# Pairing the down products of four shared pieces behind a routed loop, and moving the count of ranks

## The chip, the cores and the metric

The kernel runs on one core of one Trainium2 chip. The metric is the device time of one execution in microseconds (us), of which several runs are taken. A profile is one further execution with the hardware profiler on. Engines are called as in the profile: PE is TensorE (PEld its weight loads), DVE is VectorE, ACT is ScalarE, POOL is GpSimd, SP is SyncE.

## What is computed

1024 tokens of width 512 (two sequences of 512) go through a feed-forward part, attention, and the same feed-forward part again, each behind a layer norm and added to the stream `x`:

```python
x = x + 0.5 * ffn(layernorm(x))
x = x + attention(layernorm(x))      # 32 heads of 128, 8 key/value heads, causal
x = x + 0.5 * ffn(layernorm(x))

# ffn: a shared part and 16 routed experts, the best 2 for each token
gu_s = x2 @ shared_w_gate_up.T;  g_s, u_s = split(gu_s)          # inner width 512
shared_out = silu(g_s) * u_s @ shared_w_down.T
probs = softmax(x2 @ gate_w.T);  topk_vals, topk_idx = top_k(probs, 2)
gu = einsum('th,eih->eti', x2, w_gate_up)                        # inner width 128
out_e = einsum('eti,ehi->eth', silu(g) * u, w_down)
ffn = combine(out_e) + shared_out
```

## The kernel before

Matrix products are made in three steps from a high and a low part of each operand (`PARTS`; the parts have the type fp32r), so that one product of 128 x 512 is three matmuls a chunk of 128 inner elements. Transposes, the down product of the experts and the count of ranks are plain fp32 matmuls, which the trace shows as two records each.

The shared part of a feed-forward stage is cut into eight **pieces** (`SLOTS`): four slices of 128 of the inner width (`NSH`) times two halves of the tokens. Piece s has slice s // 2 and token half s % 2. For each piece PE runs `gate_up(n, s)` (24 matmuls: 12 into a gate bank 0 or 1, 12 into an up bank 2 or 3), ACT takes the silu (`gate`), DVE multiplies (`multiply`), ACT and DVE cut the result in two parts (`high`, `low`), PE runs `down(n, s)` (12 matmuls into banks 4 to 7, one bank a token tile), and DVE adds the four banks to `x` (`add_down`, L934). Each `down` waits bank by bank for the `add_down` of the piece before it.

Pieces 0 to 4 (`BEFORE` = 4) begin ahead of the **routed loop**, the rest comes behind it. The routed loop works off 31 tiles of 128 rows, sorted by expert. How it gets its rows: DVE picks the two experts of each token (`router`, `chosen`); PE counts with nine matmuls against `below` and `ones` how many tokens come before each one (`rank`, L1224 and L1228, put between the second and the third of the four chunks of the up product of piece 1); DVE turns this into row numbers (`place`, L878 to L889); POOL scatters the rows with 16 indirect DMAs (L490), SP loads them tile by tile (L324), and PE transposes the first one (L1239).

Behind the loop POOL gathers the results back into `yg` with 16 indirect DMAs, two for each token tile (L501); in the first feed-forward stage it makes subtractions for the attention weights between them (L524). DVE adds them to `x` with their weights (`combine`, L1015, four instructions for two token tiles). The order on each engine is written out by hand, in `feed_forward` and what follows it. In the first stage the next norm hangs on the end of this work (`statistics`, `scaled` L827, then PE's `turn_norm` L1153); in the second stage the output is stored by SP as soon as a tile is complete.

The order behind the loop on PE, before: gate/up of 5, down 4, gate/up of 6, down 5, then down 6 and gate/up of 7 (first stage) or gate/up of 7 and down 6 (second stage), down 7. Each engine goes strictly through its list, so an instruction that waits holds what stands behind it.

## Time and profile before

| | us |
|---|---|
| median of 3 runs | 1179.36 |
| lowest and highest | 1179.07, 1181.36 |
| the profiled execution, its own time | 1182.96 |
| its span, first to last instruction | 1181.3 |
| PE busy in the span | 1116.7 (95%) |
| DVE, ACT, POOL busy | 674.8, 567.6, 469.3 |

Read it from the chain of waits, which follows the work that ended last back from the end of the program, and then in the order of time at the places where the chain leaves PE. Starts are in us from the beginning of the span. The timeline joins neighbouring instructions of one kind into a row ("x4"); its duration is that of the row. The first feed-forward stage lies at 0 to 222, attention behind it to about 984, the second stage from there to the end.

### The profile page before, as it was taken

The numbers are of one execution on the slowest core, as the hardware profiler recorded it, in microseconds if no ns is written. First come the engines' busy times: TensorE is split into PE (matmuls) and PEld (weight loads), VectorE is DVE, ScalarE is ACT, GpSimd is POOL, SyncE is SP. The second block draws the span as 40 slices with busy tenths as digits, with TensorE's granted clock in tenths as the row PEclk, the third lists the DMA queues.
The fourth block names the chain that finished last, engine by engine and source line by source line (L and its number), as shares of the span: only waits on it lengthen the run. The fifth ranks groups of instructions, "written<-read, shape, count | busy, mean of one in ns | idle before, by whom it ended". The sixth has DMA issues, their size and how long they took to land.

```text
span 1181.3 us, 20221 instructions
## 1 busy us (share of the span) xinstructions
PE 1116.7 (95%) x5982; PEld 931.3 (79%) x5983; DVE 674.8 (57%) x1826; ACT 567.6 (48%) x1512; POOL 469.3 (40%) x486
## 2 busy tenths in 40 slices
PE   5989997889999999999999999999999988989996
PEld 4867775778888888888888888888888876877774
DVE  6657768755444545455445454454544456667767
ACT  3346652356445536454545454544543543356640
POOL 1456548116315325323423532522531410455543
PEclk9999999899999999999999999999999999999999
DMA  9984556101101000010110110010100017744546
GB/s 355 388 335 165 171 173 221 54 1 37 54 2 36 35 19 5 31 53 0 36 53 0 36 53 0 36 53 0 36 1 1 1 36 272 310 146 162 171 155 190
DMA packets 38603, 114.61 MB, mean 97 GB/s; under 512 B 4384, under 2 KB 4384, under 8 KB 36512
## 3 DMA queue, kind: packets, MB, share of 16 engines
q1 hardware_dynamic: 33440, 97.30, 22.8%
q0 software_dynamic: 5120, 16.78, 4.2%
q8 instruction: 22, 0.36, 0.1%
q14 instruction: 21, 0.17, 0.0%
HBM read 79.20 MB, written 34.87 MB: 97 GB/s over the span
## 4 chain that ended last, share of the span: by engine, by line
PE 84%; DVE 5%; issue 3%; ACT 3%; DMA 3%; POOL 1%; SPq 0%; DVEq 0%; ACTq 0%; POOLq 0%
PE bank L1291 23%; PE bank L1360 15%; PE bank L1376 8%; PE bank L1326 8%; PE bank L1270 6%; PE bank L1196 6%; PE bank L1304 6%; PE bank L1278 3%; PE bank L1213 2%; PE bank L1239 2%; POOL x_rows L490 1%; PE bank L1372 1%; PE bank L1322 1%; DMA experts<-in_ffn_w 1%; DVE x L1015 1%
## 5 line engine op out<-in xcount | busy, mean ns | idle before, releaser
L517 POOL TENSOR_TENSOR scores<-scores,pinv 128x512 f32<-128x512 f32 (+3 forms) x256 | 176.4, 721 | 367.0 <-DVE pinv L1052 367.0
L467 POOL TENSOR_TENSOR tback_lo<-experts,tback_hi 128x768 fp32r<-128x768 f32 x62 | 114.2, 1844 | 77.9 <-ACT tback_hi L622 77.8
L708 ACT ACTIVATE scores<-scores,nmax 128x512 f32<-128x512 f32 (+3 forms) x256 | 140.3, 558 | 0.5 <-DVE nmax L1042 0.5
L682 ACT ACTIVATE pT_hi<-bank 128x512 fp32r<-128x512 f32 (+2 forms) x192 | 86.9, 487 | 108.0 <-PE bank L1304 108.0
L720 ACT ACTIVATE oT_hi<-bank 128x512 fp32r<-128x512 f32 x64 | 38.3, 598 | 208.7 <-PE bank L1372 208.7
L1022 DVE TENSOR_TENSOR pT_lo<-bank,pT_hi 128x512 fp32r<-128x512 f32 (+2 forms) x192 | 100.8, 553 | 48.4 <-ACT pT_hi L682 48.4
L1042 DVE CUSTOM_DVE_ANT_0 scores<-bank,causal 128x512 f32<-128x512 f32 (+3 forms) x256 | 112.2, 486 | 1.5 <-issue 0.5
L1360 PE MATMUL bank<-wds_hi,oT_hi 128*128 128x512 f32 x256 | 105.9, 414 | 1.4 <-DVE oT_lo L1026 1.4
L1291 PE MATMUL bank<-xnT_hi,wqs_hi 128*128 128x512 f32 x256 | 106.4, 416 | 0.1
L1026 DVE TENSOR_TENSOR oT_lo<-bank,oT_hi 128x512 fp32r<-128x512 f32 x64 | 44.2, 691 | 108.6 <-ACT oT_hi L720 108.6
L1291 PE MATMUL bank<-xnT_lo,wqs_hi 128*128 128x512 f32 x256 | 100.8, 394 | 0.0
L1291 PE MATMUL bank<-xnT_hi,wqs_lo 128*128 128x512 f32 x256 | 100.8, 394 | 0.0
L1360 PE MATMUL bank<-wds_hi,oT_lo 128*128 128x512 f32 x256 | 100.5, 393 | 0.0
L1360 PE MATMUL bank<-wds_lo,oT_hi 128*128 128x512 f32 x256 | 99.5, 389 | 0.0
L1304 PE MATMUL bank<-ident,scores 128*128 128x128 f32 x640 | 90.8, 272 | 2.4 <-DVE pT_lo L1022 2.4
L1304 PEld LDWEIGHTS bank<-ident,scores 128*128 128x128 f32 x640 | 75.3, 141 | 11.0 <-DVE pT_lo L1022 3.0
L1062 DVE TENSOR_TENSOR x<-bank,x 128x512 f32<-128x512 f32 x64 | 44.1, 691 | 64.9 <-PE bank L1360 64.9
L1326 PE MATMUL bank<-kT_hi,qT_hi 128*128 128x512 f32 (+2 forms) x192 | 73.1, 381 | 2.2 <-DVE qT_lo L1026 2.2
L971 DVE TENSOR_TENSOR xT_lo<-bank,xT_hi 128x512 fp32r<-128x512 f32 x62 | 42.9, 691 | 51.9 <-ACT xT_hi L612 51.9
L524 POOL TENSOR_TENSOR wqs_lo<-raw_q,wqs_hi 128x512 fp32r<-128x512 f32 x32 | 41.2, 1289 | 75.4 <-ACT wqs_hi L656 75.3
L1376 PE MATMUL bank<-pT_hi,vv_hi 128*128 128x512 f32 (+2 forms) x192 | 65.5, 341 | 1.6 <-DVE pT_lo L1022 1.6
L1278 PE MATMUL bank<-experts,hT 128*128 x124 | 63.8, 595 | 1.8 <-ACT hT L633 1.8
(199 smaller groups left out, 2923.7 us busy)
## 6 DMA issues: line engine op xcount, KB each, us to landing
experts<-in_ffn_w SPq DMA_DIRECT2D x32, 768.0 KB, 11.0
xn<-x_rows SPq DMA_DIRECT2D x62, 256.0 KB, 2.7
y_rows<-xn SPq DMA_DIRECT2D x62, 256.0 KB, 2.0
raw_q<-in_wq SPq DMA_DIRECT2D x8, 1024.0 KB, 6.1
raw_d<-in_wd SPq DMA_DIRECT2D x8, 1024.0 KB, 4.9
x_rows<-experts SPq DMA_DIRECT2D x1, 7936.0 KB, 30.5
raw_w<-in_ffn_w SPq DMA_DIRECT2D x8, 768.0 KB, 6.0
raw_kv<-in_wkv SPq DMA_DIRECT2D x8, 512.0 KB, 3.3
```

The lines of the kernel that those rows point to most:

```text
L467: nc.gpsimd.tensor_tensor(tback[par][1][:], experts[:, bass.ds(at + FRONT, GU - FRONT)], tback[par][0][:].bitcast(F32), ALU.subtract).then ...
L517: nc.gpsimd.tensor_tensor(s, s, pinv[k % 2][:, i:i + 1].to_broadcast([P, P * (i + 1)]), ALU.mult).then_inc(att.normed, 1)
L682: nc.scalar.activation(pT[0][:, lo_col:hi_col], bank[b][:, 0:hi_col - lo_col], ACT.Copy).then_inc(att.t_hi, 1)
L708: nc.scalar.activation(s, s, ACT.Exp, bias=nmax[par][:, i:i + 1], scale=-1.0, accum_out=psumr[par][:, i:i + 1]).then_inc(att.exp, 1)
L1022: nc.vector.tensor_tensor(pT[1][:, lo_col:hi_col], bank[b][:, 0:hi_col - lo_col], pT[0][:, lo_col:hi_col].bitcast(F32), ALU.subtract).then ...
L1042: nc.vector.tensor_tensor_reduce(sp_[par][:, TRI[i]:TRI[i + 1]], bank[bk][:, c:c + w], causal[:, 512 - w:512], -SCORE_SCALE, 3.0e38, ALU.a ...
L1278: last = nc.tensor.matmul(bank[6 + 1 - par][:], hT[:], experts[:, bass.ds(at[k] + GU, HID)], start=True, stop=True)
L1291: last = nc.tensor.matmul(into[:], w[a][:, c, :], xnT[z][:, c, b * SEQ:(b + 1) * SEQ], start=(m == 0), stop=(m == 3 * HC - 1))
L1304: last = nc.tensor.transpose(bank[b][:, at + (i - j) * P:at + (i - j + 1) * P], sp_[par][:, TRI[i] + j * P:TRI[i] + (j + 1) * P], ident[:])
L1326: last = nc.tensor.matmul(bank[bk][:, c:c + P * (i + 1)], qT[a][:, i * P:(i + 1) * P], kT[b][z][:, 0:P * (i + 1)], start=(m == 0), stop=(m ...
L1360: last = nc.tensor.matmul(o_bank(u)[:], oT[ob][h][a][:, tile * P:(tile + 1) * P], wds[h][z][:], start=(m == 0), stop=(m == 3 * G - 1))
L1376: last = nc.tensor.matmul(bank[1][:, j * P:SEQ], vv[bu][a][:, j, :], pT[z][:, COL[j]:COL[j] + SEQ - j * P], start=(j == 0 and m == 0), sto ...
```

## The change

1. **Pairs.** Behind the routed loop the down products of pieces 4 and 6 (the first half of the tokens) are summed in one group of banks: `down` of 4 starts the accumulation and does not end it, `down` of 6 adds to it; the same for 5 and 7. `add_down` of 4 and of 5 are gone. PE's order is now gate/up of 5, down 4, gate/up of 6, the gate half of 7, down 6, the up half of 7, down 5, (the transposes of the next norm,) down 7, in both stages. Piece 7 keeps its parts in the buffers `ab[0]`, since `ab[1]` holds those of piece 5 for longer.
2. **DVE's order.** The first `combine` stands in front of the multiplication of piece 6, the second between `low` of 6 and `add_down` of 6. `add_down` of 6 comes at once behind it in both stages.
3. **Ranks.** The nine matmuls stand behind the first chunk of the up product of piece 1, three matmuls earlier, and `ones`, `below` and `chosen` have the type fp32r. POOL writes `ones` and `below` into a part of the last expert's place, and ACT copies them from there at the start, ahead of everything else on its list.

```diff
+DOWN_ORDER = (0, 1, 2, 3, 4, 6, 5, 7)
+DOWN_AT = {s: DOWN_ORDER.index(s) for s in DOWN_ORDER}
...
-        ones = sb("ones", [P, P], F32)
-        below = sb("below", [P, P], F32)
+        ones = sb("ones", [P, P], F32R)
+        below = sb("below", [P, P], F32R)
...
-                chosen = sb("chosen", [P, TT, NEXP], F32, sub)
+                chosen = sb("chosen", [P, TT, NEXP], F32R, sub)
...
+        def ab_of(s):
+
+            return ab[0 if s == SLOTS - 1 else s % 2]
...
-                sp.wait_ge(ffn[1].added, HALF * (SLOTS - 2) + t + 1)
+                sp.wait_ge(ffn[1].added, HALF * BEFORE + t + 1)
...
+            act.wait_ge(consts.below, 1)
+            nc.scalar.activation(below[:], below_f, ACT.Copy).then_inc(consts.ranks, 1)
+            nc.scalar.activation(ones[:], ones_f, ACT.Copy).then_inc(consts.ranks, 1)
             feed_forward(0)
...
                 for t in range(HALF):
                     tile = HALF * (s % 2) + t
-                    dve.wait_ge(f.d_mm, HALF * s + t + 1)
-                    wait(dve, f.added, HALF * (s - 2) + t + 1)
-                    if s >= SLOTS - 2:
+                    dve.wait_ge(f.d_mm, HALF * DOWN_AT[s] + t + 1)
+                    if s < BEFORE:
+                        wait(dve, f.added, HALF * (s - 2) + t + 1)
+                    else:
...
-                            dve.wait_ge(ffn[n].added, HALF * (SLOTS - 4) + tile + 1)
+                            dve.wait_ge(ffn[n].added, HALF * BEFORE)
...
                 low(n, BEFORE)
-                shared(n, BEFORE + 1, SLOTS - 1)
+                multiply(n, BEFORE + 1)
+                low_gu(n, NSH - 1)
+                low(n, BEFORE + 1)
+                low_dn(n, NSH - 1)
                 combine(n, 0)
+                multiply(n, SLOTS - 2)
+                low(n, SLOTS - 2)
                 combine(n, 2)
+                add_down(n, SLOTS - 2)
...
-            add_down(0, SLOTS - 2)
             then = statistics(1, 0)
...
             low(1, SLOTS - 1)
-            add_down(1, SLOTS - 2)
             combine(1, 4)
...
-                        if half == 1 and s == 1 and c == 2:
+                        if half == 1 and s == 1 and c == 1:
                             rank(n)
...
+                first, second = s == BEFORE or s == BEFORE + 1, s > BEFORE + 1
...
-                    wait(pe, f.added, HALF * (s - 1) + t + 1)
+                    if not second:
+                        wait(pe, f.added, HALF * (s - 1) + t + 1)
...
-                        last = nc.tensor.matmul(bank[4 + t][:], ab[s % 2][a][:, t * P:(t + 1) * P],
-                                                w[b][:], start=(m == 0), stop=(m == 2))
+                        last = nc.tensor.matmul(bank[4 + t][:], ab_of(s)[a][:, t * P:(t + 1) * P],
+                                                w[b][:], start=(m == 0 and not second), stop=(m == 2 and not first),
+                                                skip_group_check=True)
...
-                gate_up(n, BEFORE + 2)
+                gate_up(n, SLOTS - 2)
+                gate_up(n, SLOTS - 1, (0,))
+                down(n, SLOTS - 2)
+                gate_up(n, SLOTS - 1, (1,))
                 down(n, BEFORE + 1)
                 if n == 0:
-                    down(n, SLOTS - 2)
-                    gate_up(n, SLOTS - 1)
                     turn_norm(1, 0)
-                else:
-                    gate_up(n, SLOTS - 1)
-                    down(n, SLOTS - 2)
                 down(n, SLOTS - 1)
```

How the order moves on DVE, behind the routed loop of the second stage (`ab_lo` is `low`, `x<-bank` is `add_down`, `x<-yg` is `combine`, `sg<-sg,bank` is `multiply`). Before:

```order
L921 TENSOR_TENSOR wdn_late_lo<-raw_w,wdn_late_hi 128x512 [waits ffn1_dn_hi]
L934 SCALAR_TENSOR_TENSOR x<-bank,x 128x512 [waits ffn1_added,ffn1_d_mm] x4
L941 TENSOR_TENSOR sg<-sg,bank 128x512 [waits ffn1_u_mm,ffn1_silu]
L946 TENSOR_TENSOR ab_lo<-sg,ab_hi 128x512 [waits ffn1_act_hi]
L934 SCALAR_TENSOR_TENSOR x<-bank,x 128x512 [waits ffn1_added,ffn1_d_mm] x4
L1015 SCALAR_TENSOR_TENSOR x<-yg,wtop,x 128x512 [waits ffn1_added,gathered0]
L1015 SCALAR_TENSOR_TENSOR x<-yg,wtop,x 128x512 [waits ffn1_added,gathered1]
L1015 SCALAR_TENSOR_TENSOR x<-yg,wtop,x 128x512 [waits moe1_added] x2
```

And in the changed kernel from the same place:

```order
L933 TENSOR_TENSOR wdn_late_lo<-raw_w,wdn_late_hi 128x512 [waits ffn1_dn_hi]
L1026 SCALAR_TENSOR_TENSOR x<-yg,wtop,x 128x512 [waits ffn1_added,gathered0]
L1026 SCALAR_TENSOR_TENSOR x<-yg,wtop,x 128x512 [waits ffn1_added,gathered1]
L1026 SCALAR_TENSOR_TENSOR x<-yg,wtop,x 128x512 [waits moe1_added] x2
L954 TENSOR_TENSOR sg<-sg,bank 128x512 [waits ffn1_u_mm,ffn1_silu]
L959 TENSOR_TENSOR ab_lo<-sg,ab_hi 128x512 [waits ffn1_act_hi]
L1026 SCALAR_TENSOR_TENSOR x<-yg,wtop,x 128x512 [waits moe1_added,ffn1_added,gathered2]
L1026 SCALAR_TENSOR_TENSOR x<-yg,wtop,x 128x512 [waits moe1_added,ffn1_added,gathered3]
L1026 SCALAR_TENSOR_TENSOR x<-yg,wtop,x 128x512 [waits moe1_added] x2
L947 SCALAR_TENSOR_TENSOR x<-bank,x 128x512 [waits moe1_added,ffn1_d_mm] x4
```

Eight `x<-bank` of the eight shown before are gone (the four that are left in this place are those of piece 6, which stood further down), and the multiplication of piece 6 now stands behind the adding of the first two gathered tiles.

How the ranks move on PE, in the up product of piece 1 of the first stage. Before:

```order
L1196 MATMUL bank3<-xnT_hi,wgu_hi 128x512
L1196 MATMUL bank3<-xnT_lo,wgu_hi 128x512
L1196 MATMUL bank3<-xnT_hi,wgu_lo 128x512
L1224 MATMUL bank2<-chosen,below 128x128 [waits ffn0_mul,consts_earlier,route0_chosen]
L1228 MATMUL bank2<-chosen,ones 128x128
...
L1228 MATMUL bank2<-chosen,ones 128x16
```

In the changed kernel:

```order
L1243 MATMUL bank2<-chosen,below 128x128 [waits consts_ranks,ffn0_mul,consts_earlier,route0_chosen]
L1247 MATMUL bank2<-chosen,ones 128x128
...
L1247 MATMUL bank2<-chosen,ones 128x16
L1211 MATMUL bank3<-xnT_hi,wgu_hi 128x512
L1211 MATMUL bank3<-xnT_lo,wgu_hi 128x512
L1211 MATMUL bank3<-xnT_hi,wgu_lo 128x512
```

The three matmuls that stood ahead of the ranks now stand behind them, and the ranks wait for one semaphore more, that of ACT's two copies.

## Rows read from the trace of the kernel before

**Rows 1.** The page's part 4, the chain of waits by engine.
```profile
PE 84%; DVE 5%; issue 3%; ACT 3%; DMA 3%; POOL 1%; SPq 0%; DVEq 0%; ACTq 0%; POOLq 0%
```
**Rows 2.** Chain in order of time, the ranks, first stage: start, us, what.
```profile
37.84 0.22 PE bank L1224 x2
38.06 1.71 PE bank L1228 x16
```
**Rows 3.** Timeline of DVE there: start, us, engine, line, what, idle before and releaser.
```profile
35.18 0.29 DVE L867 TENSOR_TENSOR chosen<-hot 128x128 f32<-128x128 f32 x1
39.79 0.17 DVE L878 TENSOR_SCALAR ntile<-bank 128x16 f32<-128x16 f32 x1 [4.24 <-PE bank L1228]
```
**Rows 4.** Timeline of PE, two fp32r matmuls of 256 columns in the routed loop.
```profile
94.22 0.28 PE L1270 MATMUL bank<-tfront_hi,xT_lo 128*128 128x256 f32 x1
94.34 0.28 PE L1270 MATMUL bank<-tback_hi,xT_hi 128*128 128x256 f32 x1
```
**Rows 5.** Chain in order of time, the first tile and the experts, first stage.
```profile
66.84 2.78 DMA xn<-x_rows
...
75.37 11.91 DMA experts<-in_ffn_w
```
**Rows 6.** Timeline of PE, transposing the first routed tile, first and second stage.
```profile
69.75 0.63 PE L1239 MATMUL bank<-ident,xn 128*128 128x128 f32 x4 [2.01 <-DMA xn<-x_rows]
1041.15 0.63 PE L1239 MATMUL bank<-ident,xn 128*128 128x128 f32 x4 [0.70 <-issue]
```
**Rows 7.** Timeline of ACT at the start of the program.
```profile
7.57 0.20 ACT L544 ACTIVATE root<-rvar 128x4 f32<-128x4 f32 x1 [5.42 <-DVE rvar L813]
```
**Rows 8.** Timeline of DVE behind the routed loop, second stage.
```profile
1156.71 0.69 DVE L941 TENSOR_TENSOR sg<-sg,bank 128x512 f32<-128x512 f32 x1 [2.44 <-PE bank L1196]
...
1158.71 2.48 DVE L934 SCALAR_TENSOR_TENSOR x<-bank,x 128x512 f32<-128x512 f32 x4
1161.10 5.39 DVE L1015 SCALAR_TENSOR_TENSOR x<-yg,wtop,x 128x512 f32<-128x512 f32 x8
...
1176.09 2.48 DVE L934 SCALAR_TENSOR_TENSOR x<-bank,x 128x512 f32<-128x512 f32 x4
```
**Rows 9.** Chain in order of time, PE behind the loop, second stage.
```profile
1148.26 2.75 PE bank L1213 x12
1151.00 5.60 PE bank L1196 x24
```
**Rows 10.** Timeline of POOL, second gathers of tiles 1 and 3, second stage.
```profile
1150.31 1.18 POOL L501 DMA_INDIRECT yg<-y_rows,rows  x1 [0.30 <-issue]
...
1155.55 0.94 POOL L501 DMA_INDIRECT yg<-y_rows,rows  x1 [0.30 <-issue]
```
**Rows 11.** DMA issues, us to landing: gather of tile 3, second stage.
```profile
yg<-y_rows,rows POOLq DMA_INDIRECT x1, 3.7
```
**Rows 12.** Timeline of DVE behind the routed loop, first stage.
```profile
187.62 0.69 DVE L941 TENSOR_TENSOR sg<-sg,bank 128x512 f32<-128x512 f32 x1 [2.43 <-PE bank L1196]
...
192.21 7.67 DVE L1015 SCALAR_TENSOR_TENSOR x<-yg,wtop,x 128x512 f32<-128x512 f32 x8
...
205.09 1.62 DVE L812 TENSOR_SCALAR veps<-mv 128x4 f32<-128x4 f32 x1
```
**Rows 13.** Timeline of POOL there.
```profile
181.59 1.43 POOL L501 DMA_INDIRECT yg<-y_rows,rows  x1 [0.30 <-issue]
...
188.04 1.30 POOL L524 TENSOR_TENSOR wks_lo<-raw_kv,wks_hi 128x512 fp32r<-128x512 f32 x1
...
192.01 1.29 POOL L524 TENSOR_TENSOR wvs_lo<-raw_kv,wvs_hi 128x512 fp32r<-128x512 f32 x1
...
203.73 2.49 POOL L524 TENSOR_TENSOR wqs_lo<-raw_q,wqs_hi 128x512 fp32r<-128x512 f32 x2
```
**Rows 14.** DMA issues: the gather issued at 181.59.
```profile
yg<-y_rows,rows POOLq DMA_INDIRECT x1, 5.7
```
**Rows 15.** Timeline of PE, transposes of attention's norm.
```profile
208.82 3.67 PE L1153 MATMUL bank<-ident,xn 128*128 128x128 f32 x16 [9.57 <-DVE xn L827]
```

More of the change, by code:

```diff
@@ L177, in build @@
         loaded = sems("loaded", "x0 x1 x2 x3 gate q kv d")
-        consts = sems("consts", "mem ident below earlier counts fold zero causal0 causal")
+        consts = sems("consts", "mem ident below earlier counts fold ranks zero causal0 causal")
         NORMS = 3
@@ L202, in wait @@
             eng.wait_ge(s, value)
+        ones_f = experts[:, (NEXP - 1) * FW + HID:(NEXP - 1) * FW + HID + P]
+        below_f = experts[:, (NEXP - 1) * FW + HID + P:(NEXP - 1) * FW + HID + 2 * P]
         block = keep.enter_context(nc.Block())
+        def ab_of(s):
+            return ab[0 if s == SLOTS - 1 else s % 2]
         def down_weights(e):
@@ L426, in _ @@
             nc.gpsimd.memset(ident[:], 0.0).then_inc(consts.mem, 1)
[L427 to L428 removed]
+            nc.gpsimd.memset(ones_f, 1.0).then_inc(consts.mem, 1)
+            nc.gpsimd.memset(below_f, 1.0).then_inc(consts.mem, 1)
             nc.gpsimd.memset(earlier[:], 1.0).then_inc(consts.mem, 1)
@@ L434, in _ @@
                                     pattern=[[-1, P]], channel_multiplier=1).then_inc(consts.ident, 1)
-            nc.gpsimd.affine_select(out=below[:], in_=below[:], compare_op=ALU.is_gt, fill=0.0, base=0,
+            nc.gpsimd.affine_select(out=below_f, in_=below_f, compare_op=ALU.is_gt, fill=0.0, base=0,
                                     pattern=[[1, P]], channel_multiplier=-1).then_inc(consts.below, 1)
@@ L591, in high @@
                 wait(act, f.d_mm, 4 * (s - 1))
-                nc.scalar.activation(ab[s % 2][0][:], sg[s % 2][:], ACT.Copy).then_inc(f.act_hi, 1)
+                nc.scalar.activation(ab_of(s)[0][:], sg[s % 2][:], ACT.Copy).then_inc(f.act_hi, 1)
             def shared(n, first, last):
@@ L1186, in gate_up @@
                 wait(pe, f.mul, s - 1)
-                for half, done in ((0, f.g_mm), (1, f.u_mm)):
+                for half in halves:
                     if half == 1 and s == 2:
@@ L1199, in gate_up @@
                             m += 1
-                    last.then_inc(done, 1)
+                    last.then_inc((f.g_mm, f.u_mm)[half], 1)
             def down(n, s, tiles=range(HALF)):
@@ L1220, in rank @@
                 pe.wait_ge(consts.earlier, 1)
+                pe.wait_ge(consts.ranks, 2)
                 pe.wait_ge(ffn[n].mul, 1)
```

12 lines of the change are left out of this document (4 added, 8 removed).

## The prediction

> **What bounds the kernel now.** I read the chain of waits first. Of the span, 84% lies on PE [rows 1], so only the stretches where the chain leaves PE can give much. Going along the chain in order of time there are four of them that this change touches: the way from the ranks to the first routed tile, once in each feed-forward stage, and the work behind each routed loop. Then the timelines of PE, DVE and POOL tell what stands in these places. In the first the reader sees DVE idle for 4.24 us until PE has counted the ranks, though `chosen` was there at 35.5 [rows 3]. Behind the counting come DVE's row numbers, POOL's scatter and SP's load of the first tile, without slack: the chain goes from POOL's scatter into the load [rows 5], and PE has waited 2.01 us when it comes, in the second stage 0.70 us [rows 6]. Behind the loop it is DVE: in the second stage it works without a gap from 1158.71 to the end of the last `add_down`, which starts at 1176.09 [rows 8]; in the first stage PE stands idle for 9.57 us until DVE has the next norm ready [rows 15].
>
> **The ranks.** Three matmuls of 512 columns step behind them. Twelve such take 2.75 us [rows 9], so three take 0.7 us, and the ranks begin that much earlier; `chosen` at 35.5 is ready well before (the ranks would start at 37.84 - 0.7 = 37.1), so no new wait. The nine matmuls took 0.22 + 1.71 = 1.93 us in 18 records [rows 2], 0.107 us each. In fp32r there are nine records instead of 18. The trace has no fp32r matmul of so few columns. One of 256 columns with its own weight load takes 0.12 us from start to start [rows 4], so nine cannot be expected above 9 x 0.12 = 1.1 us, unless few columns are dear in this type, and then at worst they stay at 1.93. I take 9 x 0.107 = 0.97, a gain of 0.96 us; ends 0 and 1.0. The chain to the first tile is so shortened by 0.7 + 0.96 = 1.66 us in each stage. PE itself saves only the 0.96, and its wait of 2.01 shrinks to about 1.3; in the second stage the wait of 0.70 just vanishes, which again makes 1.66. In the first stage a load of experts is waited for later in the loop [rows 5]; it is issued behind the scatter and moves with it, and for what it may keep back I take 0.15 off. Sum: 1.5 + 1.65 = **3.15 us**, ends 1.4 and 3.3.
>
> **ACT's two copies** at the start need `below` (POOL's first few us) and load a second table. ACT waited 5.42 us before its first work at 7.57 [rows 7], and two short copies and a table load fit. If that cover were gone, the copies would hold the first norm. I cost them at nothing. POOL's work there has the same length.
>
> **The second stage behind the loop.** Two `add_down` of four instructions go. That of piece 4 stood in front of a wait of 2.44 us for PE [rows 8], and is worth nothing by itself; in its place stands the first `combine`. Tile 1 lands at 1150.31 + about 3.8 = 1154.1 [rows 10, 11]; three of the four instructions come behind that, at 5.39 / 8 = 0.67 us each [rows 8], so it ends at 1156.1. The multiplication of piece 6 started at 1156.71 and still can: slack 0.6 us. From there to the end of its `low` are 2.0 us (1158.71), as before. Where `add_down` of 5 stood, the second `combine` runs: 4 x 0.67, to 1161.4 (tile 3 landed at 1155.55 + 3.7 = 1159.3). `add_down` of 6 follows, 2.4 us, to 1163.8. PE meanwhile, at 5.60 us a gate/up and 2.75 a down [rows 9]: the gate half of 7 to 1159.4, down 6 to 1162.2, the up half to 1165.0. So DVE now waits 1.2 us for the up half: that is the stall that is late next. Then 2.0 us for multiplication and parts of piece 7 (1167.1), eight instructions of `combine` (5.3, to 1172.4), and the last `add_down` starts at 1172.4 instead of 1176.09. PE's down 5 and 7 end by 1170.5, in time. Gain: **3.7 us** (4.8 for two `add_down` less 1.1). Ends: 2.6, if gather and lists cost a little more, and 4.8, if the up half is no wait.
>
> **The first stage behind the loop.** Here the gather is slower and POOL subtracts between. The second gather of tile 1 lands at 181.59 + 5.7 = 187.3 [rows 13, 14], hardly before 187.62, when the multiplication of piece 6 ran, just behind PE's end of that piece [rows 12]. DVE instructions with both inputs in SBUF are held by POOL's subtractions: eight of `combine` took 7.67 us here and 5.39 in the second stage [rows 8, 12], and a TENSOR_SCALAR of 4 columns took 1.62 us under POOL's pair at 203.73 [rows 12, 13], where one of 16 columns takes 0.17 [rows 3]. So I count: two more of the first `combine`, one held until 188.04 + 1.30 = 189.3, end at 190.6; multiplication and high part to 191.9; `low` meets the subtraction at 192.01 and ends at 193.8. Down 6 on PE waits for it from 190.2 (187.4 and a gate half of 2.8) to 193.8: 3.6 us of new idle time, and `combine` comes after it: to 196.4, `add_down` of 6 to 198.85. Before, it followed `combine` at 199.8 and ended at 202.2. That is 3.35 us earlier for the statistics. Their scaling then falls under POOL's pair at 203.73 to 206.2, which it had missed, and loses about 1.1. **2.3 us** remain, handed on unchanged to attention: down 7, `combine` of the other half and its `add_down` keep their lengths, and PE's other waits here lie inside. Ends: 0, if PE's clock drops in the new wait and DVE meets POOL once more; 4.6, if every meeting is missed.
>
> By the Trainium skill, "SBUF — State Buffer", section "Who interferes with whom", an instruction of VectorE with two SBUF inputs and one of GpSimd that reads SBUF exclude each other for a whole instruction, and whoever comes first wins. By that rule the sum above could swing both ways by issue order alone: that is the first rival, 4.6 us in this stage if DVE wins the first meeting, 2.3 if POOL does. The durations just named agree with it.
>
> **The sum.** 3.15 + 3.7 + 2.3 = 9.15 us. Against the profiled execution's own time, 1182.96 (span 1181.3 and 1.7 around it), that gives 1173.8. This execution lies 3.6 above the median of the runs, 1179.36; less 9.15 that is **1170.2 us**. 0.2% of it, 2.4 us, is about what a measurement of this kernel can tell from no change.
>
> **Rivals.**
> - *DVE misses POOL in the first stage.* If the first `combine` gets ahead of the subtraction at 188.04, `low` of 6 is done at about 190.2, down 6 waits for nothing, and the gain there is 4.6 to 6: total 11.5 to 12.9, 1167 us. For: before, three collisions cost 2.3 + 1.4 us and nothing fixes their order. Against: the gather's landing at 187.3 puts DVE exactly onto 188.04. 0.15.
> - *The first stage gives nothing, or the ranks give half.* PE idles for 3.6 us in front of down 6; at the lower of the two clock levels its 36 matmuls to the transposes take up to twice as long, and DVE waits for the up half. Or narrow fp32r matmuls stay at 1.93 us, 1.9 less in all. Either way 5 to 7 us remain: 1173.5. For: PE ran its 16 transposes in 3.67 us after the idle time of rows 15. Against: DVE has 1 us of slack there. 0.20.
> - *Little comes through* (gain under 2.4): both tails are taken back by the new waits. It needs both of the last at once. 0.04.
> - *Slower.* DVE's list is strict, and now the first `combine` stands before the multiplication of 6, on which down 6 and everything behind hang. Each us by which the gathers of tiles 0 and 1 land later than about 1154.7 in the second stage (0.6 us later than now), and at any lateness in the first, is paid in full. To lose the 9.15 us and 2.4 more, they would have to be 6 us later in both stages. They are issued at the same place behind the loop, and landed in 3.7 and 5.7 us [rows 11, 14]. 0.03.
>
> **How the numbers follow.** The forecast, gains of 7 to 11 us, gets 0.58. Faster by over 0.2%: 0.58 + 0.15 + 0.20 = 0.93; within: 0.04; slower: 0.03. The range takes in the first two rivals up to gains of 13 and down to 5: 1166.4 to 1174.4. Left out are gains under 5 and over 13, some 0.15.
>
> **What would show it.** Right: DVE's idle time before L878's successor falls from 4.24 to about 2.6 us, with 9 records for the ranks; PE's wait for the first tile is about 1.3 us in the first stage and near 0 in the second; 16 fewer `x<-bank` instructions, DVE busy about 10 us less; in the second stage a wait of DVE of about 1 us for PE's up half, and 13.7 us instead of 17.4 from the end of `low` of 6 to the last `add_down`; in the first stage a wait of PE of 2 to 4 us at down 6, and a shorter one than 9.57 at the transposes. Wrong: a `combine` that waits beyond 187.5 or 1154.7 in those terms, ranks of 1.9 us, or an attention part that is not as long as before.

## The result, and the profile after

The changed kernel took **1174.22 us** (median of 8 runs, 1171.65 to 1177.11), the kernel before 1179.82 beside it (8 runs, 1175.92 to 1182.32): ratio 0.9952, 95% interval 0.9933 to 0.997. That is 5.6 us faster; by the interval it can be 3.5 to 7.9. Two more comparisons, below, gave 0.9953 and 0.9961. The forecast was 1170.2, 9.15 us faster. The sign was right and the gain came out 3.6 us smaller; the time lies in the range, 0.2 us from its end. One later run, of e2, took 1858.39 us at a mean granted clock of 0.559, counts in its median alone and enters no ratio.

The profiled execution of the changed kernel took 1171.97 us, with a span of 1170.3. That is 11.0 us less than the one before (1182.96, span 1181.3), twice the difference of the medians. So I first cut both spans at the same eleven events, to see what of the 11 us belongs to the change. The chain of waits by engine, the answer to [rows 1], only says that PE gave two of its hundredths to POOL:

```profile
PE 82%; DVE 5%; DMA 3%; issue 3%; POOL 3%; ACT 3%; DVEq 0%; ACTq 0%; SPq 0%; POOLq 0%
```

The stretches, each worked out from starts in the timelines of PE and DVE:

| Stretch | before | after | difference |
|---|---|---|---|
| start to the router's fold matmuls | 29.95 | 31.50 | +1.55 |
| fold to the end of the ranks, first stage | 9.81 | 6.76 | -3.05 |
| ranks to PE's first tile transposes | 29.99 | 28.87 | -1.12 |
| to the gate/up of piece 5 (the routed loop) | 103.21 | 103.49 | +0.28 |
| **tail 1**: to the next norm's transposes | 35.86 | 33.65 | -2.21 |
| to the second stage's first gate/up (attention) | 778.56 | 778.60 | +0.04 |
| to the fold | 13.74 | 12.19 | -1.55 |
| to the end of the ranks, second stage | 11.34 | 8.10 | -3.24 |
| to the first tile transposes | 28.69 | 28.99 | +0.30 |
| to the gate/up of piece 5 | 100.95 | 102.46 | +1.51 |
| **tail 2**: to the start of the last `add_down` | 33.99 | 30.49 | -3.50 |

Several of these differences lie where the change touches nothing. The 24 matmuls of the first gate/up show one source, the speed at which PE runs. At a granted clock of 1.00 (the high level, 2.4 GHz) such a piece takes 5.60 us [rows 9]. The first of each stage took, by the chain in order of time, before and then after:

```profile
16.35 7.24 PE bank L1196 x24
...
987.38 7.38 PE bank L1196 x24
```

```profile
16.95 8.19 PE bank L1211 x24
...
982.87 5.82 PE bank L1211 x24
```

In the first stage the two differ by 0.95 us, in the second by 1.56, the other way. Each begins behind a wait of PE of 2.50 to 3.93 us. Rows of single matmuls are 0.40 us long in the fast parts and 0.63 in the slow ones; slow are 7 and 8 of the 24 before, 12 and none with the change. Before, the granted clock reads 0.50 there (the lower level, 1.2 GHz): from the start in the first stage, and in the second only from 1.5 us behind it. In the first stage of the changed kernel it reads 1.00 although the matmuls are as slow, so there the reading doesn't explain them.

**The ranks** in the first stage of the changed kernel: the chain, and DVE's timeline in front of them (start, us, engine, line, operation; in brackets the idle time before it and what ended it).

```profile
37.15 0.27 PE bank L1243
37.41 0.86 PE bank L1247 x8
```

```profile
36.74 0.29 DVE L879 TENSOR_TENSOR chosen<-hot 128x128 fp32r<-128x128 f32 x1
...
38.29 0.17 DVE L890 TENSOR_SCALAR ntile<-bank 128x16 f32<-128x16 f32 x1 [1.18 <-PE bank L1247]
```

There are now 9 records in the first stage where there were 18 [rows 2]. They begin 0.06 us behind the end of `chosen` (36.74 + 0.29 = 37.03), and DVE waits 1.18 us for them instead of 4.24 [rows 3].

**The first tile.** PE's timeline, and the load that the chain names:

```profile
67.13 0.63 PE L1258 MATMUL bank<-ident,xn 128*128 128x128 f32 x4 [0.21 <-DMA xn<-x_rows]
...
88.24 0.66 PE L1258 MATMUL bank<-ident,xn 128*128 128x128 f32 x4 [2.39 <-DMA xn<-x_rows]
```

```profile
77.79 10.40 DMA xn<-x_rows
```

PE's wait for the first tile is 0.21 us, where it was 2.01 [rows 6]. In the second stage it is 0.35, where it was 0.70. In the first stage this wait differs much between profiles of one kernel (1.63 us in e1, 2.25 in e9), so that the 0.21 is not the change's alone. Later in the first loop a tile's load takes 10.40 us and lands at 88.19; that it queues behind the loads of the last experts is my reading. Before, the last of the experts was waited for until 87.28 [rows 5]. The wait has changed its name and not its place; the loop is as long as it was.

**Tail 2**, DVE's timeline:

```profile
1151.28 2.72 DVE L1026 SCALAR_TENSOR_TENSOR x<-yg,wtop,x 128x512 f32<-128x512 f32 x4
1153.93 2.47 DVE L947 SCALAR_TENSOR_TENSOR x<-bank,x 128x512 f32<-128x512 f32 x4
1157.58 0.69 DVE L954 TENSOR_TENSOR sg<-sg,bank 128x512 f32<-128x512 f32 x1 [1.18 <-PE bank L1211]
...
1159.58 5.61 DVE L1026 SCALAR_TENSOR_TENSOR x<-yg,wtop,x 128x512 f32<-128x512 f32 x8
1165.10 2.48 DVE L947 SCALAR_TENSOR_TENSOR x<-bank,x 128x512 f32<-128x512 f32 x4
```

From the start of the second `combine` (1151.28) to the start of the last `add_down` (1165.10) there are 13.8 us. The forecast had 13.7, with a wait of 1.1 to 1.2 us for the up half, and here it is 1.18.

**Tail 1**, DVE's timeline and POOL's subtractions beside it, and PE's first work behind it:

```profile
184.01 3.45 DVE L1026 SCALAR_TENSOR_TENSOR x<-yg,wtop,x 128x512 f32<-128x512 f32 x3 [0.60 <-DMA yg<-y_rows,rows]
...
188.75 0.69 DVE L959 TENSOR_TENSOR ab_lo<-sg,ab_hi 128x512 fp32r<-128x512 f32 x1 [0.70 <-ACT ab_hi L601]
189.36 4.05 DVE L1026 SCALAR_TENSOR_TENSOR x<-yg,wtop,x 128x512 f32<-128x512 f32 x4
...
195.85 2.47 DVE L817 BATCH_NORM_STATS2 stats<-x 128x6 f32<-128x512 f32 x4
...
198.63 0.17 DVE L824 TENSOR_SCALAR veps<-mv 128x4 f32<-128x4 f32 x1
...
200.31 5.26 DVE L839 TENSOR_SCALAR xn<-x,mv,rstd 128x512 f32<-128x512 f32 x4
```

```profile
185.60 1.30 POOL L533 TENSOR_TENSOR wks_lo<-raw_kv,wks_hi 128x512 fp32r<-128x512 f32 x1
...
189.56 1.31 POOL L533 TENSOR_TENSOR wvs_lo<-raw_kv,wvs_hi 128x512 fp32r<-128x512 f32 x1
...
200.02 0.94 POOL L510 DMA_INDIRECT yg<-y_rows,rows  x1 [0.30 <-issue]
200.99 2.48 POOL L533 TENSOR_TENSOR wqs_lo<-raw_q,wqs_hi 128x512 fp32r<-128x512 f32 x2
```

```profile
204.27 3.68 PE L1168 MATMUL bank<-ident,xn 128*128 128x128 f32 x16 [6.11 <-DVE xn L839]
```

The statistics begin at 195.85, 25.2 us behind the gate/up of piece 5, where they began 29.35 us behind it before. But then the scaling of the norm (L839), which takes 1.92 us by itself, takes 5.26, until POOL's last pair of subtractions is done (200.99 + 2.48 = 203.47). PE's transposes follow 0.8 us later. The scaling's row begins 0.7 us ahead of the pair, but within the issue of POOL's last gather (200.02 to 200.96), which the pair follows without a gap.

### The profile page after: what moved, and what is told of

Same layout as the page of the kernel before. It is cut to its first block, busy times and chain, and to the rows that moved or that the text cites. A ratio compares the mean times of both kernels' runs of the same rounds, so it can differ in the third digit from the quotient of the medians.

```text
span 1170.3 us, 20160 instructions
## 1 busy us (share of the span) xinstructions
PE 1110.9 (95%) x5964; PEld 926.4 (79%) x5965; DVE 668.2 (57%) x1810; ACT 569.7 (49%) x1515; POOL 467.5 (40%) x486
## 4 chain that ended last, share of the span: by engine, by line
PE 82%; DVE 5%; DMA 3%; issue 3%; POOL 3%; ACT 3%; DVEq 0%; ACTq 0%; SPq 0%; POOLq 0%
PE bank L1310 23%; PE bank L1379 15%; PE bank L1395 9%; PE bank L1345 8%; PE bank L1289 7%; PE bank L1323 6%; PE bank L1297 4%; PE bank L1211 4%; PE bank L1258 2%; POOL yg L510 1%; PE bank L1230 1%; PE bank L1391 1%; POOL x_rows L499 1%; PE bank L1341 1%; DMA xn<-x_rows 1%
```

## The experiments

Twelve experiments ran, with nine kernels: the change repeated (e1, e9), one part alone or undone (e2 to e4), and one thing moved (e5 to e8, e12). e10 and e11 repeat e5 and e6, since the answers of one chip could not be read in full. The tails' lengths are compared as in the table above.

**e1, the changed kernel again, unchanged.**

> The changed kernel once more, unchanged: a second profile and more times. Its first profiled execution (span 1170.3) was 11.0 us shorter than that of the kernel before, the medians of eight runs differ by 5.6. Forecast's theory: the change is worth about 9 us, and the profiled pair holds some 2 us more of clock and load luck: here the four stretches that it touches (router's fold to first tile transposes; gate/up of piece 5 to the next norm's transposes; the same two in the second stage) should again be about 35.6, 33.7, 37 and 30.5 us long (before 39.8, 35.9, 40.0 and 34.0), and the median 1170 to 1172. Rival, the slower half of its runs is the rule: one of these stretches is 3 to 5 us longer in this profile, with a new wait in it, or a low clock behind PE's new wait at down 6; median 1174 to 1176.

Measured: 1173.57 us (12 runs) beside 1179.44 of the kernel before (33 runs), ratio 0.9953 (0.9941 to 0.9966). Tail 1 was 33.53, tail 2 30.98; fold to ranks 6.76 in both stages; fold to first tile 37.02 and 35.95. So the stretches are nearly as short again, and the median is still only 5.9 us below, between the 1170 to 1172 of the theory and the rival's 1174 to 1176. The spread within the kernel goes with the clock: its run at a mean granted clock of 0.984 took 1178.31 us, the three at 0.992 or more took 1172.16 to 1173.49. Over 86 runs (this kernel twice, the three below, the kernel before) a straight line within each kernel gives 0.55 us for each 0.001 of clock; the means of the clock differ by no more than 0.0015 between these kernels, so it blurs the comparison and does not decide it.

**e2, the ranks' part alone**, on the kernel before:

```
-                        if half == 1 and s == 1 and c == 2:
+                        if half == 1 and s == 1 and c == 1:
                             rank(n)
...
-        ones = sb("ones", [P, P], F32)
+        ones = sb("ones", [P, P], F32R)
```

(and `below` and `chosen` alike, with ACT's two copies)

> The kernel before with the ranks' part alone: one chunk earlier, in fp32r, with ACT's two copies. Forecast's theory: 3.15 us faster, 1.5 in the first stage and 1.65 in the second; nine rank matmuls in about 1.0 us; the tails behind the loops as before (35.9 and 34.0 us). Rival, the DMA queue sets the first loop's pace (the last loads of experts or a tile queued behind them land at 87 to 88 us in both profiles so far, whatever the ranks do): the first stage gives under 0.5 us, 1.7 to 2 in all, with PE's first tile transposes earlier but the gate/up of piece 5 where it was. Rival, ACT's copies or the extra table load delay the start: the router's fold begins 1.5 us later, as in the changed kernel's profile (31.50 against 29.95), and then 0 to 1.5 us in all.

Measured: 1177.66 us beside 1179.44, ratio 0.9985 (0.9972 to 0.9998). The forecast's 3.15 us (0.9973) lies inside, as does half of it. Fold to ranks took 6.75 us in the first stage and 8.10 in the second, where the granted clock was 0.75. Tail 1 was 34.91 (35.86 before), tail 2 34.00 like before.

**e3, the pairing alone**: the changed kernel with the ranks as before.

```
-                        if half == 1 and s == 1 and c == 1:
+                        if half == 1 and s == 1 and c == 2:
                             rank(n)
...
-                pe.wait_ge(consts.ranks, 2)
```

> The changed kernel with the ranks as before (fp32, behind the second chunk, no copies on ACT): the pairing alone, in both stages. Forecast's theory: 6.0 us faster than before, 3.7 in the second stage's tail (34.0 to about 30.3 us) and 2.3 in the first (35.9 to 33.6), more by 1 to 2 where DVE misses POOL's subtractions. Rival: the first stage's tail gives under 0.5 us, because the next norm's scaling now runs into POOL's last subtractions and PE's new wait is followed by a low clock; 3.5 to 4 us in all. If the start is late by the copies on ACT, it is not late here (fold at 29.9 to 30.2).

Measured: 1177.48 us, ratio 0.9992 (0.9981 to 1.0002). **This is far from the 6.0 us of the forecast**: even the interval's end is 2.2 us. Tail 1 was 33.58, tail 2 31.93. The tails are shorter than before, by 2.3 and 2.1, but in the twelve runs hardly 2 us of it show. Here is the end of DVE's list in this kernel's tail 2, and POOL's last gather:

```profile
1165.56 0.75 DVE L1020 SCALAR_TENSOR_TENSOR x<-yg,wtop,x 128x512 f32<-128x512 f32 x1 [0.49 <-DMA yg<-y_rows,rows]
1167.29 2.08 DVE L1020 SCALAR_TENSOR_TENSOR x<-yg,wtop,x 128x512 f32<-128x512 f32 x3 [0.98 <-DMA yg<-y_rows,rows]
1169.29 2.48 DVE L941 SCALAR_TENSOR_TENSOR x<-bank,x 128x512 f32<-128x512 f32 x4
```

```profile
1161.86 1.38 POOL L507 DMA_INDIRECT yg<-y_rows,rows  x1 [0.30 <-issue]
```

DVE now waits for rows of the last two tiles, 0.49 and 0.98 us, a wait that is in no profile of an unpaired kernel. It is in that of e1 too:

```profile
1163.28 2.08 DVE L1026 SCALAR_TENSOR_TENSOR x<-yg,wtop,x 128x512 f32<-128x512 f32 x3 [0.65 <-DMA yg<-y_rows,rows]
```

and in those of e4 (0.23 and 0.97), e9 (0.72) and e10 (0.79). The last gather of e3 is issued at 1161.86, 20.2 us behind the first; in the changed kernel's first profile it was 18.9. POOL's issues of 0.95 us take 1.3 to 1.4 here four times.

**e4, the ranks one chunk earlier, but in fp32**, else the changed kernel.

```
-        ones = sb("ones", [P, P], F32R)
+        ones = sb("ones", [P, P], F32)
```

> The changed kernel with ranks in fp32 (18 records, no copies on ACT), but one chunk earlier as there. Forecast's theory: between the pairing alone and the whole change: 0.7 us a stage faster than the former, 0.96 a stage slower than the latter; 18 records in 1.93 us. Rival, narrow fp32 matmuls cost no more than the narrow fp32r ones once PE runs at the high clock: no difference to the changed kernel.

Measured: 1175.99 us, ratio 0.9965 (0.9952 to 0.9977), between e3 and the whole change as the forecast's theory said. Its interval overlaps that of e1 (0.9941 to 0.9966), and lies just below that of e3; by the ratios e4 is 3.2 us faster than e3, where the one chunk in each stage should give 1.4. The stretches tell the parts apart. From the fold of the first stage, the ranks begin after 6.19 us in e3 and 5.59 here, both at a granted clock of 1.00: **one chunk is worth 0.6**. They last 2.08 and 2.18 us here and in e3, 1.17 and 1.07 in fp32r: **fp32r is worth 0.9 to 1.0**. Tail 1 was 35.11 us in this profile, no shorter than e2's 34.91 without the pairing.

**What tells 33.5 from 35.1 us.** The same happens in e9, which is the changed kernel itself. In e9's profile, DVE and POOL in tail 1:

```profile
188.53 1.99 DVE L959 TENSOR_TENSOR ab_lo<-sg,ab_hi 128x512 fp32r<-128x512 f32 x1 [0.69 <-ACT ab_hi L601]
...
199.75 3.57 DVE L824 TENSOR_SCALAR veps<-mv 128x4 f32<-128x4 f32 x1
...
204.83 1.92 DVE L839 TENSOR_SCALAR xn<-x,mv,rstd 128x512 f32<-128x512 f32 x4
```

```profile
188.69 1.27 POOL L533 TENSOR_TENSOR wvs_lo<-raw_kv,wvs_hi 128x512 fp32r<-128x512 f32 x1
...
199.38 0.94 POOL L510 DMA_INDIRECT yg<-y_rows,rows  x1 [0.30 <-issue]
200.34 2.49 POOL L533 TENSOR_TENSOR wqs_lo<-raw_q,wqs_hi 128x512 fp32r<-128x512 f32 x2
```

In the first profile `low` of piece 6 began at 188.75 and was through 0.1 us ahead of the subtraction at 189.56. Here its row begins 0.16 us ahead of the one at 188.69, and yet it loses to it and takes 1.99 us instead of 0.69; e4 shows the same (0.15 us ahead, 1.99 us). From there DVE is 1.3 us late, and the addition of eps (L824), not the scaling, is caught by the last gather and the pair: 3.57 us instead of 0.17. The pair ends at 202.83 and the transposes begin 2.6 us behind it, where it was 0.8. That is the unpaired kernels' distance: in e2, POOL's pair ends at 203.66 and PE starts at 206.27. So whichever way it falls, **POOL's pair sets the end of tail 1**, and POOL's list is the same in all kernels (pair 25.9 us behind the first gather before, 25.9 and 25.5 in the two profiles of the change). The rest of the study tests this.

**e5, POOL's last two subtractions late.** They move behind the first stage's last down product:

```
-                    if n == 0 and t >= HALF - 1:
+                    if n == 0 and HALF - 1 <= t < TT - 1:
                         first_cuts(low_part, t - HALF + 1, t - HALF + 2)
...
-            first_cuts(low_part, HALF + 1)
...
+            pool.wait_ge(ffn[0].added, HALF * (BEFORE + 2))
+            first_cuts(low_part, HALF)
             att_slots(pool, slot)
```

> The changed kernel, but POOL makes its last two subtractions (wqs_lo 2 and 3) only when DVE has added the last down product of the first stage, so behind the next norm's scaling. In four profiles the transposes of the next norm start 0.8 us behind the end of that pair where DVE's scaling runs into it, and 2.6 behind where the addition of eps does. Theory, the pair's end sets the end of the first stage's tail in the changed kernel: the tail (gate/up of piece 5 to the transposes) goes from 33.6 to about 30.3 us, the time 3.3 us down, to 1170.3. Rival, something else comes last right behind it (gathers of the second half, PE at low clock after its idle time, wqs_lo wanted earlier): under 1 us, and a new wait in attention's first 50 us.

Measured: ratio 0.9928 (0.9907 to 0.9949), but on a chip on which the kernel before took 1197.59 us, so 1170.3 could not come out. Tail 1 was 30.45 us (expected 30.3), and attention 778.64 (778.60 in the changed kernel), so nothing is lost behind it. The end of this tail, DVE, POOL and PE:

```profile
211.00 2.54 DVE L840 TENSOR_SCALAR xn<-x,mv,rstd 128x512 f32<-128x512 f32 x4
```

```profile
210.69 0.95 POOL L510 DMA_INDIRECT yg<-y_rows,rows  x1 [0.30 <-issue]
```

```profile
211.94 3.68 PE L1169 MATMUL bank<-ident,xn 128*128 128x128 f32 x16 [3.12 <-DVE xn L840]
```

The pair is away, and the scaling still takes 2.54 us and not 1.92, and PE starts 0.30 us behind the end of the last gather's issue (211.64). e8 shows the same two numbers. So the issue of a gather holds this instruction too, for 0.6 us, and is what ends last now. That would also explain how the pair could catch instructions that began 0.6 to 0.7 us ahead of it: the gather in front of it held them already.

**e6, the same without the pairing.**

> The same shift of POOL's last pair in the kernel with the ranks' part alone, so without the pairing. Theory, the pair only holds the addition of eps here (1.60 us instead of 0.17): 1.4 us down, the tail from 34.9 to 33.5, time 1176.2. The pairing is then worth 3.3 us in the first stage with the pair out of the way (this against the kernel before this one), where it is worth 0 to 1.8 with it. Forecast's theory had put 2.3 there with the pair in its place. Rival, the pairing gives nothing in this stage for another reason: the two kernels' tails are alike again.

Measured: 1203.56 us beside 1197.59, ratio 1.0047. Tail 1 was 36.06 us with a wait of DVE of 3.88 us for PE in front of piece 6, tail 2 42.90. Inconclusive: this chip adds waits whose releaser the profile does not show ("remote"). Two instructions of the `add_down` of piece 5 in tail 2:

```profile
1173.99 0.69 DVE L941 SCALAR_TENSOR_TENSOR x<-bank,x 128x512 f32<-128x512 f32 x1 [2.16 <-remote]
1178.28 0.69 DVE L941 SCALAR_TENSOR_TENSOR x<-bank,x 128x512 f32<-128x512 f32 x1 [3.59 <-remote]
```

Repeated as e11.

**e7, DVE's last list of the second stage in another order** (tile 4's rows ahead of the multiplication of piece 7, and so on).

```
-            multiply(1, SLOTS - 1)
-            low(1, SLOTS - 1)
-            combine(1, 4)
-            combine(1, 6)
-            add_down(1, SLOTS - 1)
+            gather_add(4, 0)
+            gather_add(4, 1)
+            multiply(1, SLOTS - 1)
+            gather_add(5, 0)
+            low(1, SLOTS - 1)
+            gather_add(5, 1)
+            gather_add(6, 0)
+            down_add(4)
+            gather_add(6, 1)
+            down_add(5)
+            down_add(6)
+            gather_add(7, 0)
+            gather_add(7, 1)
+            down_add(7)
```

> The changed kernel with DVE's last list of the second stage in another order: the additions of tile 4 stand ahead of the multiplication of piece 7, one of tile 5 ahead of its low part, then the down products of tiles 4 to 6 are added before tile 7's rows, so that behind the last gather's landing three additions are left instead of seven. Theory, the tail is set by both DVE's waits for PE (1.2 and 0.7 us) and POOL's sixteen gathers (the last lands some 5 us after its issue at 1157.9 to 1161.9): last addition ends 2 us earlier relative to the gate/up of piece 5 (about 31.4 instead of 33.5 us), and runs with slow gathers lose less. Rival, DVE's work alone sets it and the gaps can't be filled because rows land too late: under 0.7 us.

Measured: ratio 0.9966 (0.9946 to 0.9986) on the same chip. In this order the additions of the last down product don't stand together, so tail 2 is taken here to the end of the last addition: 39.31 us, with a wait "remote" of 7.97 in it, so it says nothing on the order. (In the three profiles of the changed kernel this length is 32.97, 33.46 and 33.77.) Tail 1, unchanged in this kernel, was 33.49.

**e8, both.**

> Both of the last changes in one, late subtractions in the first stage and the other order in the second stage's tail. If each is worth what its theory says and neither touches the other: 3.3 + 2.0 = 5.3 us below the changed kernel, 1168.3. Rival: clock and DMA in between take back what comes earlier, 1170 or more.

Measured: 1187.41 beside 1197.59, ratio 0.992 (0.9894 to 0.9946). Tail 1 was 30.73 us, tail 2 to the end of the last addition 38.63 with "remote" waits too. 5.3 us below the changed kernel would have been 0.991 by its ratio elsewhere, which is inside the interval; so is e5's ratio, so the two are not told apart.

**e9, the changed kernel** once more, on a chip like the first.

> The changed kernel unchanged, as the kernel to compare the next three with on the same chip (the four before ran on a chip that gave the kernel before 1197.6 us and showed waits whose releaser the profile doesn't name, so that only their stretches can be read). Tail of the first stage 33.5 us, of the second 30.5 to 32 on an undisturbed chip; ratio to the kernel before 0.995.

Measured: 1175.31 beside 1179.31, ratio 0.9961 (0.9944 to 0.9977). Tail 1 was 35.14 us, as shown above, and not 33.5; tail 2 31.29.

**e10, late subtractions**, the kernel of e5.

> The late subtractions alone once more, beside the changed kernel. Tail of the first stage 30.4 us again (30.45 and 30.73 on the other chip). Theory: 3.0 us faster than the changed kernel. Rival: what is gained at the transposes is lost in attention's first 50 us or by a lower clock, under 1 us in the time.

Measured: 1171.01 us, ratio 0.9927 (0.9909 to 0.9946): **4.3 us below the changed kernel beside it**, where the theory said 3.0 and the intervals, each some 2 us either way, allow it. Its own profile had a tail 1 of 32.68 us and not 30.4: DVE waited 3.40 us for the first rows (2.26 in the changed kernel's first profile) and so met POOL's subtraction of 191.87 with `low`. Nor is the clock the same here: its mean was 0.9913 over the six runs of e10 and 0.9879 over the seven of e9. By the 0.55 us of e1's line 1.9 of the 4.3 us go with it, and 2.4 are left; whether the clock is cause or companion, the runs don't tell.

**e11, late subtractions without the pairing**, the kernel of e6.

> Late subtractions without the pairing, once more, since a wait of 1.4 us of DVE for PE hid the answer on the other chip. Theory: tail of the first stage 33.5 us (34.9 less 1.4), so that the pairing is worth 3.1 there once the pair of subtractions is out of the way; with the late pair 6 us slower than the paired one, of which 3 come from the second stage. Rival: tail 31 to 32, the pairing worth little in either case.

Measured: 1176.99 us, ratio 0.9975 (0.996 to 0.9991). Tail 1 was 33.49 us, expected 33.5, tail 2 33.99. DVE in tail 1:

```profile
202.33 0.17 DVE L819 TENSOR_SCALAR veps<-mv 128x4 f32<-128x4 f32 x1
...
204.00 1.92 DVE L834 TENSOR_SCALAR xn<-x,mv,rstd 128x512 f32<-128x512 f32 x4
```

The addition of eps takes 0.17 us again. Against e5 and e8 (30.45 and 30.73, on the other chip) the pairing is worth 2.9 us in tail 1 with the pair away, against e10 (32.68, on this one) 0.8. e11 is 6.0 us slower than e10, as expected, with a mean clock of 0.9874 against 0.9913, by the same line 2.1 of the 6.0.

**e12, subtractions grouped and late, and the new order in tail 2** (with the edits of e8; what differs from them is shown).

```
-                    if n == 0 and t >= HALF - 1:
-                        first_cuts(low_part, t - HALF + 1, t - HALF + 2)
+                    if n == 0 and t == HALF - 1:
+                        first_cuts(low_part, 0, 1)
+                    if n == 0 and t == HALF + 1:
+                        first_cuts(low_part, 1, HALF)
```

> All together: POOL's subtractions of wvs and wqs 0 and 1 in one group behind the gathers of tile 5 (under DVE's add_down and statistics, which ran at their usual 2.47 us beside a subtraction in every profile so far), the last two late, and DVE's other order in the second stage's tail. Theory: the second combine of the first stage takes 2.7 instead of 4.05 us, the tail 29.1 us (4.4 below the changed kernel), the second stage's tail 2 us below it: 6 us in all. Rival: gathers of tiles 6 and 7 land later by the grouped subtractions and hold the second half's combine, or PE's project of wvs waits: no better than the late subtractions alone.

Measured: **1168.74 us** (5 runs, 1166.41 to 1173.31), ratio 0.9904 (0.989 to 0.9919): the lowest median, 6.6 us below the changed kernel beside it and 10.6 below the kernel before. Its interval overlaps that of e10, and its mean clock was 0.9916, which by the line is 2.0 of the 6.6 us. Its profile is of the slowest of the five runs (1173.31), and neither half of the theory shows in it. Tail 2, to the end of the last addition, was 33.29 us (32.97 to 33.77 in the three profiles of the changed kernel), with the widest gathers of all (20.6 us from first to last):

```profile
1163.73 0.75 DVE L1164 SCALAR_TENSOR_TENSOR x<-yg,wtop,x 128x512 f32<-128x512 f32 x1 [1.75 <-DMA yg<-y_rows,rows]
...
1166.86 1.53 DVE L1164 SCALAR_TENSOR_TENSOR x<-yg,wtop,x 128x512 f32<-128x512 f32 x2
1168.50 0.69 DVE L1171 SCALAR_TENSOR_TENSOR x<-bank,x 128x512 f32<-128x512 f32 x1
```

Behind the last rows there are only two additions and one down product left, and the wait of 1.75 us stands earlier, at tile 6. The last addition ends 8.3 us behind the start of the last gather's issue, where it was 9.2 to 9.8 in those three, so the order is worth some 1 us measured from the gathers, and the wider gathers took that back here. The 2 us of the theory are not shown. Tail 1 was 33.54 us, not 29.1. The grouped subtractions began under the second `combine` and not behind it, and all three held it:

```profile
189.95 6.56 DVE L1029 SCALAR_TENSOR_TENSOR x<-yg,wtop,x 128x512 f32<-128x512 f32 x4
```

```profile
191.53 1.29 POOL L535 TENSOR_TENSOR wvs_lo<-raw_kv,wvs_hi 128x512 fp32r<-128x512 f32 x1
192.76 2.53 POOL L535 TENSOR_TENSOR wqs_lo<-raw_q,wqs_hi 128x512 fp32r<-128x512 f32 x2
```

6.56 us for four additions that take 2.7. Where the 6.6 us of the medians come from, this profile doesn't show. The late pair with the subtractions where they were (e5's tail 1) and this order of tail 2 make e8; it was only run on the chip with the "remote" waits, so whether it is better is open.

## Why the prediction was right, and where it was off

Its sum was 9.15 us: 3.15 for the ranks, 3.7 and 2.3 for the tails. What the profiles show:

- **The ranks: 3.15 forecast, 3.0 in the profiles.** At a granted clock of 1.00, fold to ranks takes 8.25 to 8.27 us in e3 and 6.75 to 6.77 with the change, 1.5 a stage, against 1.66. With the change it is 8.10 us where the clock was 0.75 or 0.76 (second stage of the first profile) and 9.64 where it was 0.60 (second stage of e9), so a single profile can hide the gain. fp32r was sized by records of 0.107 us at 0.97, and measured 0.9 to 1.0. The chunk was sized at 0.7 and is 0.6, because of a wrong statement: "`chosen` at 35.5 is ready well before ..., so no new wait". That was read in a profile in which PE had run this stretch at the low clock, 7.73 us from the fold to the ranks; in e3 it is 6.19. Now `chosen` comes last, by 0.1 us. For the same reason DVE's wait of 4.24 us fell to 1.18 and not to 2.6: without the low clock it was 2.69 (e3). By times alone the part is worth 1.8 us (e2) with an interval from 0.2 to 3.3.
- **ACT's copies** cost nothing that shows. ACT's first work of the norm began at 7.65 us with them and at 7.57 before. On the undisturbed chips the router's fold began between 28.58 and 31.50 us in seven profiles with the copies, and between 29.95 and 31.10 in the three without.
- **Second stage's tail: 3.7 forecast, 2.7 measured.** Unpaired it took 33.99, 34.00 and 33.99 us; paired, on undisturbed chips and in the old order, 30.49, 30.98, 31.93, 31.71, 31.29 and 31.14, a mean of 31.26. In the first of these every number of the forecast's step stands (1.18 of wait, 13.8 us). The step missed what is late next behind that wait: it placed DVE's last eight additions by DVE alone, and did not ask when the last of POOL's sixteen gathers lands. With DVE 3.5 us earlier it does matter: in five of the six paired profiles DVE waits there for rows, 0.65 to 1.47 us, and tail 2 less these waits is 30.3 to 30.6 us in all six, 3.4 to 3.7 below the unpaired ones.
- **First stage's tail: 2.3 forecast, 2.2 between the two first profiles, 0 or 1.3 against e2.** That the first number fits is luck: two errors cancel in it. The statistics came 4.1 us earlier and not 3.35, since `low` of 6 got ahead of the subtraction; the addition of eps was no longer held, 1.45 us more (1.62 and 0.17), a term that the sum lacks; and the scaling lost 3.35 us (5.26 against 1.92) and not 1.1. The step that failed is this last one: "Their scaling then falls under POOL's pair at 203.73 to 206.2, which it had missed, and loses about 1.1". The step took DVE's instructions as sliding earlier one by one with a charge for each meeting. They don't slide: POOL's last gather and the pair come at a nearly fixed time of its list (the pair begins 29.8 to 30.8 us behind the gate/up of piece 5 in all eight profiles that have it there), a TENSOR_SCALAR that meets them stands until they are done, and the tail ends 0.8 us behind the pair or, if DVE is a little later, 2.6 us. Six profiles of paired kernels with the pair in its old place gave 33.65, 33.53, 33.58 and 33.49, or 35.11 and 35.14. Unpaired there are only two such profiles, 34.91 in e2 and 35.86 before, where the eight additions met POOL more often (7.67 us against 6.97); which of the two is the rule isn't shown. Moving the pair (e5 and e8 against e11) gave a pairing worth 2.9 us in this tail, in e10 0.8.

By the profiles that makes 3.0 + 2.7 + some 0.8 (34.91 less the mean of the six, 34.08) = 6.5 us, against 4.0 to 5.9 in three measurements whose intervals reach up to 6.6, 7.0 and 7.9. The first rival, that DVE misses POOL and gains 4.6, occurred in no profile as a whole: in four of the six `low` of 6 did get past the subtraction, and the pair took the gain back. DVE is busy 6.6 us less (668.2 against 674.8) where about 10 were forecast, as the time for which it is held counts as busy. The second came nearest: 5 to 7 us, 1173.5, because the first stage gives nothing. It had the right place and the wrong cause, a low clock of PE behind the new wait at down 6 (1.66 us in the first profile, 3.05 in e9). It was given 0.20, too little: the text held all that decided it, a DVE that comes earlier and a POOL that does not move.

By the Trainium skill, "SBUF — State Buffer", section "Who interferes with whom", not only instructions with two SBUF inputs contend with GpSimd, but also those that run in a two-port mode, which `tensor_scalar` can enter, and the one that comes later is blocked for the whole instruction. The traces agree, once POOL's last gather is counted in: the TENSOR_SCALARs at L839 and L824 began within its issue, 0.6 to 0.7 us ahead of the pair, and stood still through both (5.26 and 3.57 us), while BATCH_NORM_STATS2 and the additions from a bank took their 2.47 us beside a subtraction in every profile. Read so, the rule spoke against the 2.3 us.

Not settled: e2 and e3 give 1.8 and 0.9 us by their ratios (1.8 and 2.0 by the medians), the whole change 5.5. e4 against e3 gives 3.2 us for the one chunk, whose stretches show 1.2, so e3 is the odd one: its tails are 2.3 and 2.1 us shorter and its time hardly shows it. Whether the parts help one another or the intervals of some 1.5 us each way hide a plain sum, these runs don't tell. Nor was it tried why POOL issues some gathers in 1.2 to 1.5 us instead of 0.95. DVE's work may have a part in it: over the fourteen profiles it was so in 44 of the 118 issues that began within a `combine`, and in 19 of the other 330.

## What to carry to other kernels

Where two engines exclude each other, moving work earlier on one of them is worth only what the other's fixed list allows: look for the last meeting in front of the consumer, and move that instruction first (here POOL's last pair: 3 us of tail 1 in two of three profiles). When a wait is taken out of a list, place every remaining input of the list by its own engine's time, the last DMA above all. And cut two profiles at common events before believing their difference: of the 11.0 us here 4 to 5 were the luck of two executions. Measure a stretch to the same event in every kernel, too: where an order changes, "the last `add_down`" is another instruction.

## What the runs showed of the hardware

- How fast PE runs behind the same wait differs from execution to execution: 12 matmuls of a projection early in attention, each time behind a wait of 1.41 us, took 3.07 us at a granted clock of 1.00 (before and changed), 4.42 at 0.66 (e2) or 5.49 at 0.50 (e4), the 24 of the first gate/up of a stage 5.8 to 8.4. The runs of one kernel spread over 7 us, and the long ones go with a lower mean clock.
- Beside BATCH_NORM_STATS2 and SCALAR_TENSOR_TENSOR with one input in a bank POOL's subtractions cost nothing; beside TENSOR_SCALAR, even of 4 columns, they cost their whole length, with the gather's issue in front of them up to 3.4 us for an instruction of 0.17. The issue of a gather alone holds a TENSOR_SCALAR as well: 0.6 us of the scaling in e5 and e8, 0.4 of the addition of eps in e10 (0.58 against 0.17).
- One of the chips ran the kernel before in 1197.6 us instead of 1179.4. Its profiles show DVE idle for up to 8 us and ACT for up to 10.8 until a releaser that the profile does not name, at places that differ between kernels, and ranks to first tile took 36.0 to 38.7 us instead of 28.5 to 31.8. What it waits for was not found.
